# Gated scan and capacity-routed experts on one core: routing ahead of low halves in the last group, expert rows normalised by VectorE, last expert finished by tile

## What is computed

```python
x = x + layernorm(attn(layernorm(x)))          # 16 x 1024 x 256 float32
x = x + layernorm(ffn(layernorm(x)))
# attn: g = sigmoid(x Wg^T + bg);  h[t] = (1-g[t]) h[t-1] + g[t] x[t];  h Wo^T + bo
# ffn, N = 16384 tokens, E = 8 experts, C = 320 slots, H = 1024:
eid   = argmax(softmax(xf @ router_w + router_b))
rank  = cumsum(onehot(eid))[token, eid] - 1;   valid = rank < C
buf[eid, rank] = xf where valid                # first 320 tokens of each expert
y     = relu(buf @ w1 + b1) @ w2 + b2          # per expert
yov   = relu(xf @ ow1 + ob1) @ ow2 + ob2       # overflow, for all other tokens
out   = y[eid, rank] if valid else yov
```

## Time and profile before

| | |
|---|---|
| median of 3 executions | 1218.23 us (1217.35 to 1219.71) |
| the profiled execution's own time | 1216.73 us |
| its span in the trace | 1215.0 us |
| TensorE busy (share of the span) | 1152.8 us (95%) |
| VectorE | 1012.0 us (83%) |
| ScalarE | 733.8 us (60%) |
| GpSimd | 726.4 us (60%) |
| groups, roughly | up to 1050 us |
| experts, roughly | 1055 to 1198 us |

### The profile page before, as it was taken

How to read it: one execution, slowest core, us unless ns; L and a number is a source line. 1 busy time by engine, 2 the same in 40 slices (tenths; PEclk the granted TensorE clock), 3 DMA queues, 4 the chain that set the end, 5 groups by cost and what they waited for, 6 DMA issues and landing times.

```text
span 1215.0 us, 24627 instructions
## 1 busy us (share of the span) xinstructions
PE 1152.8 (95%) x7657; PEld 1031.3 (85%) x7657; DVE 1012.0 (83%) x2758; ACT 733.8 (60%) x1296; POOL 726.4 (60%) x855
## 2 busy tenths in 40 slices
PE   5489999999999999999999999999999999899994
PEld 4378888888888888888888888888888888889994
DVE  4688888889888998889889888888889977678882
ACT  3256666656656665666666656556566666577772
POOL 4465656656666556565656666666565664256774
PEclk8799999999999999999999999999999999999997
DMA  8211111111111111111111011101111100344520
GB/s 252 87 43 38 53 49 46 41 37 35 35 35 35 35 35 35 35 35 35 35 35 35 18 34 35 35 20 32 35 35 35 35 18 18 109 144 155 175 87 27
DMA packets 59431, 65.06 MB, mean 54 GB/s; under 512 B 7835, under 2 KB 55629, under 8 KB 59268
## 3 DMA queue, kind: packets, MB, share of 16 engines
q1 hardware_dynamic: 52228, 59.32, 15.1%
q0 software_dynamic: 7168, 5.32, 1.5%
HBM read 40.17 MB, written 38.61 MB: 65 GB/s over the span
## 4 chain that ended last, share of the span: by engine, by line
PE 84%; DVE 5%; POOL 5%; issue 3%; ACT 2%; DMA 0%; DVEq 0%; POOLq 0%; ACTq 0%
PE psY L1122 11%; PE psY L1125 10%; PE psY L1124 10%; PE psH L1022 10%; PE psH L1024 10%; PE psH L1023 10%; PE psA L1022 5%; PE psA L1024 5%; PE psA L1023 5%; PE psT L1078 3%; POOL tok L410 2%; PE psT L1035 2%; DVE st L695 2%; POOL rstd L369 1%; PE psT L1084 1%
## 5 line engine op out<-in xcount | busy, mean ns | idle before, releaser
L369 POOL TENSOR_TENSOR rstd<-veps,mhalf 128x4 f32<-128x4 f32 (+1 forms) x144 | 195.6, 1358 | 386.6 <-DVE nmean L707 386.6
L536 ACT ACTIVATE hid<-psH,biasT 128x512 f32<-128x512 f32 (+2 forms) x320 | 206.3, 645 | 270.0 <-PE psH L1024 262.1
L1122 PE MATMUL psY<-W_hi,hid_hi 128*128 128x256 f32 x1200 | 347.4, 290 | 0.3 <-DVE hid_lo L841 0.3
L1125 PE MATMUL psY<-W_hi,hid_lo 128*128 128x256 f32 x1200 | 339.8, 283 | 0.0
L1124 PE MATMUL psY<-W_lo,hid_hi 128*128 128x256 f32 x1200 | 339.5, 283 | 0.0
L1022 PE MATMUL psH<-xfT_hi,W_hi 128*128 128x512 f32 (+2 forms) x640 | 241.6, 377 | 3.0 <-DVE xfT_lo L785 3.0
L1024 PE MATMUL psH<-xfT_hi,W_lo 128*128 128x512 f32 (+2 forms) x640 | 240.1, 375 | 0.0
L1023 PE MATMUL psH<-xfT_lo,W_hi 128*128 128x512 f32 (+2 forms) x640 | 239.9, 375 | 0.0
L841 DVE TENSOR_TENSOR hid_lo<-hid,hid_hi 128x512 fp32r<-128x512 f32 (+2 forms) x320 | 202.3, 645 | 42.8 <-ACT hid_hi L540 29.2
L1122 PEld LDWEIGHTS psY<-W_hi,hid_hi 128*128 128x128 f32 x1200 | 227.4, 189 | 9.8 <-DVE hid_lo L841 1.5
L1124 PEld LDWEIGHTS psY<-W_lo,hid_hi 128*128 128x128 f32 x1200 | 227.6, 190 | 6.6
(11 more groups left out here) (110 smaller groups left out, 2089.6 us busy)
## 6 DMA issues: line engine op xcount, KB each, us to landing
xin<-L_attn_x SPq DMA_DIRECT2D x32, 512.0 KB, 3.5
stage<-L_ffn_w SPq DMA_DIRECT2D x16, 1024.0 KB, 6.3
out<-outt SPq DMA_DIRECT2D x31, 512.0 KB, 2.9
xbuf<-zrow SPq DMA_DIRECT2D x1, 2570.0 KB, 18.1
xin<-xbuf SPq DMA_DIRECT2D x8, 257.0 KB, 5.7
stage<-L_ffn_ow SPq DMA_DIRECT2D x2, 1024.0 KB, 10.2
xbuf<-x,idx POOLq DMA_INDIRECT x128
b_b<-L_ffn_b SPq DMA_DIRECT2D x1, 1024.0 KB, 13.4
```

The source lines that it names most:

```text
L369: pool.tensor_tensor(rstd[k][:, t0:n], veps[k][:, t0:n], mhalf[:, t0:n], ALU.pow).then_inc(s_rs[k], 1)
L536: act.activation(hid[j % 2][:, at:n], psH[:, j % 2, at:n], ACT.Relu, bias=bias).then_inc(s_hid, 1)
L1122: pe.matmul(psY_t[:, t, :], hi, w[0][:, j, :], start=(j == 0 and t % 2 == 0), stop=False, skip_group_check=True)
L1125: last = pe.matmul(psY_t[:, t, :], lo_, w[0][:, j, :], start=False, stop=(j == HC - 1), skip_group_check=True)
```

## The change

- **Last group.** TensorE computes `route` first, and `rank` right after layer1(1), ahead of the loop over j. VectorE does `choose` before lo(0) and `place` before lo(1), and reads the rows of expert (0, 0) after lo(6) instead of after lo(7). ScalarE copies the logits out before its first relu. The transposes of expert (0, 0)'s rows stand between layer2(6) and layer2(7).
- **Normalisation.** The rows of the last group and of all experts are normalised by VectorE (`norm2` there), after the recurrence's place for the last group, after lo(7) for expert (0, 0), and after lo(5) in an expert's step. GpSimd keeps the deviation; its `residual3` moves up by that, and `keep_rows` now waits for VectorE's tok2.
- **Last expert.** VectorE normalises and adds tile by tile (`last_rows`), each tile with a semaphore count of its own, and GpSimd issues each tile's indirect DMA on that; the cast of the token numbers comes before.
- **SyncE.** The store of the last group is queued after expert 2's row and W1 loads.

```diff
@@ -323,7 +325,6 @@
...
             load_w2((0, 1))
-            store((NG // 2 - 1, 1))
@@ -332,6 +333,8 @@
...
                 load_w1(far)
+                if not live(grp(i, u, -1), E):
+                    store((NG // 2 - 1, 1))
                 sp.wait_ge(s_we_hi, cnt(nxt, 8, 8))
@@ -400,14 +403,16 @@
...
-            def norm2(g, src, n, base=0):
-                i, v = g
-                deviation(2, g, n, base)
-                pool.wait_ge(s_nm[2], cnt(g, 1, 1) + base)
-                pool.wait_ge(s_T1, cnt(g, 2, 0) + 2 * base)
+            def norm2(g):
+                i, v = g
+                deviation(2, g, TG)
+                if not live(grp(i, v, 1), NG):
+                    return
+                pool.wait_ge(s_nm[2], cnt(g, 1, 1))
+                pool.wait_ge(s_T1, cnt(g, 2, 0))
                 pool.sem_inc(s_held, 1)
-                for t in range(n):
-                    last = pool.tensor_scalar(tok2[:, t, :], src[v][:, t, 0:D], rstd[2][:, t:t + 1],
+                for t in range(TG):
+                    last = pool.tensor_scalar(tok2[:, t, :], x1[v][:, t, 0:D], rstd[2][:, t:t + 1],
                                               nmr[2][:, t:t + 1], ALU.mult, ALU.add)
@@ -460,6 +465,7 @@
...
                     pool.wait_ge(s_out, cnt((NG // 2 - 1, v), 1, 1))
+                pool.wait_ge(s_tok2, cnt(e, 1, 1) + NG)
                 pool.sem_inc(s_held, 1)
@@ -472,15 +478,23 @@
...
                     .then_inc(s_out, 1)
+                rows_of(e)
+
+            def rows_of(e):
+                i, v = e
                 pool.tensor_copy(oidx[v][:].unsqueeze(2), x1[v][:, 0:ET, D:ROW]).then_inc(s_oidx, 1)
...
                 i, v = e
-                pool.wait_ge(s_out, cnt(e, 1, 1) + NG)
+                tail = not live(grp(*e, 1), E)
+                if not tail:
+                    pool.wait_ge(s_out, cnt(e, 1, 1) + NG)
                 pool.wait_ge(s_oidx, cnt(e, 1, 1))
...
                     n = min(P, C - t * P)
+                    if tail:
+                        pool.wait_ge(s_tail_out, t + 1)
                     pool.indirect_dma_start(out=out_rows, out_offset=bass.IndirectOffsetOnAxis(oidx[v][0:n, t:t + 1], 0),
@@ -490,7 +504,7 @@
...
                 if live(nxt, E):
-                    norm2(nxt, xe, ET, NG)
+                    deviation(2, nxt, ET, NG)
                 if live(prev, E):
@@ -499,10 +513,10 @@
...
             last_group, last_expert = (NG // 2 - 1, 1), (E // 2 - 1, 1)
-            norm2((0, 0), xe, ET, NG)
+            deviation(2, (0, 0), ET, NG)
             keep_rows((0, 0))
             deviation(3, last_group, TG)
-            norm2((0, 1), xe, ET, NG)
+            deviation(2, (0, 1), ET, NG)
             keep_rows((0, 1))
@@ -512,8 +526,10 @@
...
                 estep(E // 2 - 1, u)
+            pool.wait_ge(s_pre, cnt(last_expert, 1, 1))
+            pool.wait_ge(s_fin[1], landed(grp(*last_expert, -2), ET))
+            rows_of(last_expert)
             deviation(3, last_expert, ET, NG)
-            residual3(last_expert)
             store_rows(last_expert)
@@ -606,8 +622,10 @@
...
+                if not up:
+                    logits_out(now)
                 hidden(range(0, 1))
-                if run:
+                if up and run:
                     logits_out(now)
@@ -682,7 +700,6 @@
...
                 estep(E // 2 - 1, u)
-            norm3((E // 2 - 1, 1), ET, NG)
@@ -872,6 +889,26 @@
...
+            def norm2(g, src, n, base=0):
+                i, v = g
+                dve.wait_ge(s_nm[2], cnt(g, 1, 1) + base)
+                dve.wait_ge(s_T1, cnt(g, 2, 0) + 2 * base)
+                for t in range(n):
+                    last = dve.tensor_scalar(tok2[:, t, :], src[v][:, t, 0:D], rstd[2][:, t:t + 1], nmr[2][:, t:t + 1],
+                                             ALU.mult, ALU.add)
+                last.then_inc(s_tok2, 1)
+
+            def last_rows(e):
+                i, v = e
+                dve.wait_ge(s_nm[3], cnt(e, 1, 1) + NG)
+                dve.wait_ge(s_pre, cnt(e, 1, 1))
+                dve.wait_ge(s_fin[v], landed(grp(i, v, -2), ET))
+                for t in range(ET):
+                    dve.tensor_scalar(ysb[:, t, :], ysb[:, t, :], rstd[3][:, t:t + 1], nmr[3][:, t:t + 1], ALU.mult,
+                                      ALU.add).then_inc(s_tail_z, 1)
+                    dve.wait_ge(s_tail_z, t + 1)
+                    dve.tensor_tensor(outt[v][:, t, :], ysb[:, t, :], x1[v][:, t, 0:D], ALU.add).then_inc(s_tail_out, 1)
+
             def read_rows2(e):
@@ -886,8 +923,14 @@
...
-                low(0, 1)
-                if run:
+                if not up:
+                    choose(now)
+                    low(0)
+                    place(now)
+                    low(1)
+                else:
+                    low(0, 1)
+                if run and up:
                     choose(now)
@@ -907,9 +950,14 @@
...
                 else:
+                    if up:
+                        norm2(nxt, x1, TG)
                     for j in range(4 * u, 4 * u + 4):
...
                 low(6)
+                if run and not up:
+                    read_rows2((0, 0))
+                    moments(2, (0, 0), ET, NG)
                 next_x = grp(i, u, 3)
@@ -919,12 +967,10 @@
...
                 if run and not up:
-                    read_rows2((0, 0))
-                    moments(2, (0, 0), ET, NG)
+                    norm2((0, 0), xe, ET, NG)
+                    xf_lo((0, 0), C, NG)
                 if run:
                     result(now, ob2_b[:].unsqueeze(1), TG, t0=sure(now))
-                if run and not up:
-                    xf_lo((0, 0), C, NG)
                 if run:
@@ -986,6 +1032,8 @@
...
                             moments(2, nxt, ET, NG)
+                        if j == 5:
+                            norm2(nxt, xe, ET, NG)
                         if j == HC - 1:
@@ -1000,6 +1048,7 @@
...
             stats3((E // 2 - 1, 1), ET, NG)
+            last_rows((E // 2 - 1, 1))
@@ -1132,6 +1181,13 @@
...
                     pe.wait_ge(s_xf_lo, cnt(now, 2, 2))
+                if run and not up:
+                    route(now)
+                    layer1(now, 0, GT, W1[1])
+                    logits_by_token(now)
+                    layer1(now, 1, GT, W1[1])
+                    rank(now)
+                elif run:
                     layer1(now, 0, GT, W1[1], at=sure(now) * P)
@@ -1146,18 +1202,20 @@
...
                     if run:
-                        if j == 3:
+                        if j == 3 and up:
                             rank(now)
...
                     transposes1(nxt, TG)
-                if run:
+                elif run:
+                    layer2(now, HC - 2, TG, W2[1])
+                    transposes1((0, 0), ET, NG)
+                    layer2(now, HC - 1, TG, W2[1])
+                if run and up:
                     layer2(now, HC - 2, TG, W2[1], t0=sure(now))
                     layer2(now, HC - 1, TG, W2[1], t0=sure(now))
-                if not up:
-                    transposes1((0, 0), ET, NG)
```

More of the change, by code:

```diff
@@ L231, in sandwich_kernel @@
         s_fin = sems("s_fin")
+        s_tail_z = sem("s_tail_z")
+        s_tail_out = sem("s_tail_out")
         EL1 = cnt((NG // 2, 0), HC, 0)
@@ L430, in step @@
                     renumber(nxt)
-                    norm2(nxt, x1, TG)
+                    norm2(nxt)
                 if live(now, NG):
@@ L441, in _ @@
             deviation(1, (0, 0), TG)
-            norm2((0, 0), x1, TG)
+            norm2((0, 0))
             state_lo((0, 1))
```

## The result

The changed kernel's median is 1213.81 us over six executions (1212.57 to 1215.21), against 1217.79 for the kernel before over six beside it (1216.99 to 1219.71). The ratio is 0.9963, 95% interval 0.9953 to 0.9974: 4.0 us faster by the medians, 4.5 by the ratio. The forecast was 1213.0 and "faster". The profiled execution took 1212.57 us with a span of 1210.8, 4.2 less than the span before.

What follows compares the result with a forecast made beforehand. TensorE, busy 95% of the span, was taken as the bound; its idle time, slow clock and tail could be won. Terms summed to -5.2 us, 1218.2 to 1213.0, range 1206.0 to 1216.5.

Steps and rivals of the forecast that it cites:

- The last group's transposes: Last group: VectorE's normalised rows are done before TensorE comes free, -1.7 us, or -1.2 if VectorE is late.
- Route and rank: Last group: TensorE's queue waits for the one-hot at rank, ahead of layer1(2), +1.4 us (+1.2 to +1.8).
- From the last group to expert (0, 0): Up to expert (0, 0)'s layer2(0): earlier rows, partly paid back waiting for lo(0), -3.1 us (-3.5 to -2.2).
- Expert 0 to 1: Transposes for the next expert: rows come sooner, idle time shrinks and the clock is kept, -3.2 us (-3.6 to -2.6).
- Experts 1 to 6: GpSimd's add moves up behind lo(4), holds a W_lo and delays the rows, +0.72 us each, +4.3 (+2.1 to +6.6).
- the slower rival: Experts' transposes: idle stretches near 2.0 us drop the clock to 1.2 GHz in each expert, 1225.7 us; chance 0.07.
- The last expert: After the last nmr: tile-by-tile work on VectorE brings the first output DMA sooner, -2.9 us (-2.5 to -3.4).
- the held W_lo is harmless: Rival, experts 1 to 6: the add comes later or gives way, -2.6 us instead of +4.3, 1206.1 us; chance 0.2.
- the last group gives nothing: Rival: the first three terms, -3.4 us together, come to nought, 1216.4 us; chance 0.13.

Runs made afterwards that it cites:

- s_store: The changed kernel with SyncE's store of the last group back ahead of expert 2's loads: 1215.13 us, ratio 0.9972 to the kernel before.
- p_pool: The changed kernel with GpSimd again normalising the rows of experts 2 to 7, ahead of its 128x768 add: 1208.17 us, ratio 0.9918 to the kernel before.
- k_add: The changed kernel with only GpSimd's 128x768 add moved, to wait for the running expert's last lo: 1206.48 us, ratio 0.9899 to the kernel before.
- j_norm4: The changed kernel with VectorE's normalisation of an expert's rows behind lo(4) instead of lo(5): 1208.99 us, ratio 0.9929 to the kernel before.
- r_route: The changed kernel with the old order of route, rank, choose and place in the last group: 1213.94 us, ratio 0.9961 to the kernel before.
- h_all: The changed kernel with j_norm4's edit, rank behind layer1(2), expert 0's transposes behind layer2(7) and the group's result ahead of xf_lo: 1208.82 us.
- b_best: The changed kernel with k_add's edit, rank behind layer1(2), expert 0's transposes behind layer2(7) and the group's result ahead of xf_lo: 1204.35 us.

## Why the prediction was right, step by step

**The last group's transposes** stood as forecast. VectorE's rows lie before TensorE comes free; the four W_lo and two lo behind them make lo(6) late by 0.23.

**Route and rank.** The wait at rank was 0.99, not 1.2 to 1.5. The forecast took VectorE's sums to end 3.82 after layer1(0) starts, as before. But route's four matmuls now stand between layer2(7) and layer1(0), which gives VectorE that much more of a start. TensorE's timeline, kernel after:

```profile
1024.09 0.62 PE L1133 MATMUL psT<-xfT_hi,rw 128*16 128x512 f32 x2
...
1025.01 0.39 PE L1071 MATMUL psH<-xfT_hi,W_hi 128*128 128x512 f32 x1
```

That is 0.92 us (1025.01 less 1024.09), and the one-hot was there 4.34 after layer1(0) instead of 5.36. With the 0.23 for lo(6), which the forecast had not priced, and 0.4 that the two places took beyond these waits, the term is +1.6 and inside its bounds. That it is close to +1.4 is partly luck.

**From the last group to expert (0, 0): a mis-sized step.** -2.5 instead of -3.1, inside its bounds of -3.5 to -2.2. VectorE's timeline, kernel after, beside the earlier trace rows:

```profile
1045.27 1.07 DVE L712 BATCH_NORM_STATS2 st<-xin 128x6 f32<-128x256 f32 x3
...
1047.00 0.16 DVE L724 TENSOR_SCALAR nmean<-mv 128x3 f32<-128x3 f32 x1
1047.07 0.68 DVE L858 TENSOR_TENSOR hid_lo<-hid,hid_hi 128x512 fp32r<-128x512 f32 x1
1048.81 1.06 DVE L897 TENSOR_SCALAR tok<-xin,rstd,nmr 128x256 f32<-128x256 f32 x3 [1.05 <-POOL nmr L374]
```

The sums began at 1045.27, as forecast (1045.30). From nmean to the use of nmr it took 1.65 (1047.16 to 1048.81), not 1.24, beside lo(7), which the bounds had allowed for; and tok took 1.06, not 0.70. Together these are 0.8 us. The clock did stay up, and the wait for lo(0) that pays it back came, 1.31 against some 1.6. These are windows of the kernel after (columns as in the earlier trace rows); the first begins just after the idle 1.70 us and holds the idle 1.31, the second covers the waits of experts 0 to 6:

```profile
1050.00:1060.00 10.00, 8.69 (x64) 8.29 (x65) 8.34 (x24) 6.54 (x14) 2.73 (x3) 1.00 0.13 34
1060.00:1190.00 130.00, 121.23 (x911) 117.02 (x911) 108.04 (x270) 98.52 (x208) 71.76 (x67) 1.00 0.40 130
```

**Expert 0 to 1.** Right: the wait fell from 2.21 to 0.38 and the clock was kept. The way to the transposes became 1.75 shorter, not 1.94, with tok dearer than forecast, and from there to the next column it took 3.92 (1066.78 to 1070.70) instead of 5.45. The forecast had expected 4.16 there, which is not the full pace, as the next paragraph shows. The gain needs the moved store; s_store shows what it costs if that is left out.

**Experts 1 to 6.** The mechanism is the forecast's, and p_pool and k_add show it from both sides: the add falls behind lo(4), the W_lo lasts 2.22, and TensorE waits. That the size, +4.8, is so near +4.3 is partly luck: deviations offset each other. Tok cost 0.35 more per expert; in expert 4 to 5 the place grew by 0.92, not 0.72. Against that, one expert lacked the held W_lo. VectorE's, GpSimd's and TensorE's timelines, expert 3 to 4:

```profile
1117.31 2.00 DVE L858 TENSOR_TENSOR hid_lo<-hid,hid_hi 128x320 fp32r<-128x320 f32 x1 [0.23 <-ACT hid_hi L556]
...
1117.14 1.82 POOL L479 TENSOR_TENSOR outt<-ysb,x 128x768 f32<-128x768 f32 x1
...
1119.36 0.39 PE L1171 MATMUL psY<-W_hi,hid_hi 128*128 128x256 f32 x1 [1.39 <-DVE hid_lo L858]
```

Here the add got ahead of lo(4), as the slower rival supposed. It did not add to the other wait but took its place: 1.39 us at a layer2 column and none at the transposes, and this step grew by 0.55 only, the least of the six. The steps between the waits were also 0.04 to 0.22 shorter than before in the last five of the six steps. The prediction took the W_lo that the add holds behind lo(6) in the kernel before for hidden; it is not quite. lo(7) stands behind it, and TensorE's layer2(7) starts 0.25 us after the matmul ahead of it and the next one 0.23 later, where 0.12 is the pace. The timelines of VectorE and TensorE in the kernel before, beside the earlier trace rows:

```profile
1144.93 0.48 DVE L841 TENSOR_TENSOR hid_lo<-hid,hid_hi 128x320 fp32r<-128x320 f32 x1
...
1145.21 0.28 PE L1125 MATMUL psY<-W_hi,hid_lo 128*128 128x256 f32 x1
1145.46 0.39 PE L1122 MATMUL psY<-W_hi,hid_hi 128*128 128x256 f32 x1
```

That is the 0.24 between 4.16 and 3.92. At two of the other experts it was smaller, and with the change it is gone.

The Trainium skill (SBUF — State Buffer, who interferes with whom) has this exclusion for VectorE's instructions with two inputs in SBUF, and also for a tensor_scalar in its two-port fast mode. For W_lo and hid_lo the traces agree (2.22 and 2.00 beside the add, 0.68 and 0.48 without), and so they do for the tensor_scalars in j_norm4 (2.58 beside the add, 1.05 without).

**The last expert.** 2.9 forecast, 2.9 measured; a normalisation of one tile is 0.41 and not 0.29, and the handovers and the step to the DMA (0.80, not 0.88) were together 0.1 shorter, which is luck.

**The rivals.** That the held W_lo is harmless is refuted by its row and by k_add. That the last group gives nothing fell with the first three terms at -2.8. The fall of the clock in every expert did not come: the waits stayed at 1.3 to 1.6 us, and the granted clock at 1.00 in the second window above (the 2.4 GHz level). That rival's condition, an idle stretch near 2.21 us, is not what decides: the clock stayed up after 3.00 us in r_route and fell after 1.40 in h_all.

## What to carry to other kernels

Before work is moved between engines to shorten a wait, look at what the giving engine does next: its next instruction moves up, and here that cost more than the handed-over work had gained. A long add on GpSimd belongs beside instructions with nothing urgent behind them; a single wait that puts it there was worth more than the whole change. And parts of one change are to be measured singly: here the tail gave 2.9 us, the routing that names it nothing, and VectorE's normalisation won time in the last group and the first experts and lost it in the other six.

## What the runs showed of the hardware that was not expected

- A per-partition scalar of a VectorE tensor_scalar costs a fixed 0.06 us, and the rest runs at twice the rate of tensor_tensor: 0.26 us for 512 elements more, where hid_lo needs 0.20 for 192 more (0.68 and 0.48).
- GpSimd's one-input work beside a run of VectorE's two-input work was much longer: `keep_rows`, 0.83 in k_add (at 1141.99), took 3.44 in j_norm4 (at 1137.69, beside W_lo, lo and xfT_lo). In the kernel after an indirect DMA's issue took 3.82 (at 1018.70, beside W_lo, lo and xfT_lo) and the next one 0.97. No wait of TensorE was traced to these, so what they cost is not known.
- The same instructions with the same waits ran at a granted clock of 0.50 in one kernel and 1.00 in another (h_all and b_best, 1052 to 1054), which by itself moved a layer2 by 1.39 us.
